# Attention products of each softmax in one run on TensorE: a transformer layer on one Trainium2 core

## The reference, cut to what matters

```
x = x + attn(layernorm(x))              # 16 heads of 32, rotary, causal softmax
x = x + cross(layernorm(x), ctx_2048)   # 16 heads of 32, int8-like rounding of the input and output projections
x = x + experts(layernorm(x))           # 64 experts, the best 8 for each token, 128 places in each
```

```
att = softmax(q @ k.T / sqrt(32));  y = att @ v      # for each of 32 sequences and 16 heads
```

## Time and profile before

| | us |
|---|---|
| median of 3 runs | 1783.19 |
| the three runs | 1784.44, 1783.19, 1775.75 |
| span of the profiled execution | 1569.0 |
| TensorE busy in it | 1406.8 |
| VectorE busy | 1168.0 |
| ScalarE busy | 971.5 |
| GpSimd busy | 673.1 |

### The profile page before, as it was taken

How to read it: one execution, slowest core, us unless ns; L and a number is a source line. 1 busy time by engine, 2 the same in 40 slices (tenths; PEclk the granted TensorE clock), 3 DMA queues, 4 the chain that set the end, 5 groups by cost and what they waited for, 6 DMA issues and landing times.

```text
span 1569.0 us, 35603 instructions
## 1 busy us (share of the span) xinstructions
PE 1406.8 (90%) x10963; PEld 1063.2 (68%) x10996; DVE 1168.0 (74%) x3111; ACT 971.5 (62%) x3345; POOL 673.1 (43%) x654
## 2 busy tenths in 40 slices
PE   3699999999999999999999999998619887888895
PEld 2467777777777777777777777776516565655573
DVE  5678889998999989999899999889524444444453
ACT  3357777777777777777777777777504333333342
POOL 0012444444444344453444534544343544555566
PEclk9799999999999999999999999999759999999997
DMA  9861332322111100111010111000597999999964
GB/s 283 347 237 35 131 125 101 105 98 107 66 46 45 34 27 27 34 34 40 27 27 27 34 43 30 27 21 21 191 331 214 292 249 287 281 276 281 261 99 51
DMA packets 159738, 195.81 MB, mean 125 GB/s; under 512 B 39541, under 2 KB 121845, under 8 KB 159680
## 3 DMA queue, kind: packets, MB, share of 16 engines
q1 hardware_dynamic: 120768, 157.27, 30.9%
q0 software_dynamic: 38912, 37.87, 11.8%
HBM read 127.60 MB, written 130.29 MB: 164 GB/s over the span
## 4 chain that ended last, share of the span: by engine, by line
PE 65%; DMA 23%; issue 5%; DVE 4%; ACT 1%; POOL 1%; SPq 1%; POOLq 0%; DVEq 0%
PE bank L502 33%; DMA out<-x,slots 20%; PE bank L527 7%; PE bank L484 7%; PE bank L520 5%; PE bank L534 4%; PE bank L508 3%; PE bank L540 2%; PE bank L515 2%; DMA x_in<-in_x 1%; PE bank L489 1%; DMA wide_b<-in_xkT_w 1%; POOL routed L1753 1%; DMA probsT<-in_oT_w 1%; ACT probs L966 1%
## 5 line engine op out<-in xcount | busy, mean ns | idle before, releaser
L966 ACT ACTIVATE probs<-bank,small 128x128 f32<-128x128 f32 x1024 | 362.1, 377 | 51.0 <-DVE small L1269 47.8
L1753 POOL DMA_INDIRECT routed<-row,slots x248 | 252.7, 1019 | 133.8 <-issue 74.0
L1822 POOL DMA_INDIRECT out<-x,slots x128 | 199.3, 1557 | 197.6 <-DMA out<-x,slots 137.4
L1718 POOL TENSOR_TENSOR small<-small,half 128x1 f32<-128x1 f32 x96 | 54.4, 567 | 523.3 <-DVE small L1241 523.3
L966 ACT ACTIVATION_READ_ACCUMULATOR probs<-bank,small 128x1 f32 x1024 | 220.7, 216 | 0.0
L960 ACT ACTIVATE probsT<-bank 128x512 f32<-128x512 f32 x256 | 144.1, 611 | 89.1 <-PE bank L527 89.1
L1269 DVE TENSOR_REDUCE small<-bank 128x4 f32<-128x512 f32 x256 | 166.7, 682 | 35.4 <-PE bank L520 35.4
L527 PE MATMUL bank<-idf,probs 128*128 128x128 f32 x1024 | 147.2, 277 | 2.4 <-ACT probs L966 2.4
L1673 DVE TENSOR_SCALAR slots<-pairs 128x1 uint32<-128x1 f32 x128 | 13.7, 149 | 174.7 <-DMA out<-x,slots 171.1
L527 PEld LDWEIGHTS bank<-idf,probs 128*128 128x128 f32 x1024 | 122.2, 144 | 26.8 <-DVE probs L1278 3.5
L1199 ACT ACTIVATE xn<-bank 128x192 f32<-128x192 f32 x64 | 21.3, 332 | 146.4 <-PE bank L906 146.4
(11 more groups left out here) (242 smaller groups left out, 3843.4 us busy)
## 6 DMA issues: line engine op xcount, KB each, us to landing
w_gate_up<-in_w_gate SPq DMA_DIRECT2D x128, 192.0 KB, 3.8
w_gate_up<-in_w_up SPq DMA_DIRECT2D x128, 192.0 KB, 4.0
w_down<-in_w_down SPq DMA_DIRECT2D x128, 192.0 KB, 4.4
routed<-empty_row SPq DMA_DIRECT2D x4, 5120.0 KB, 22.8
x_in<-in_x SPq DMA_DIRECT2D x32, 256.0 KB, 2.6
ctx_sb<-in_ctxT_in SPq DMA_DIRECT2D x32, 256.0 KB, 3.0
x_res<-in_x SPq DMA_DIRECT2D x32, 256.0 KB, 2.6
out<-x SPq DMA_DIRECT2D x32, 256.0 KB, 2.0
```

What stands on the lines that cost most here:

```text
L966: last = act.activation(probs[:, g, j * P:(j + 1) * P], bank[:, b, j * P:(j + 1) * P], ACT.Exp, bias=negated[:, h:h + 1], **({"accum_out": ...
L1753: pool.indirect_dma_start(routed, bass.IndirectOffsetOnAxis(ap=slots_of(m)[:, k:k + 1], axis=0), row_of(m)[:, :], None, bounds_check=SLOTS ...
L1822: pool.indirect_dma_start(out.rearrange("b p (h c) -> (b p h) c", h=2), bass.IndirectOffsetOnAxis(ap=place_of[k % 2][:, half_:half_ + 1], ...
```

## The change

Two calls in TensorE's list change their place. Every instruction, wait and buffer stays as it is.

```
                 if has(cur - 5):
                     positions(cur - 5)
-                if has(cur - 4):
-                    weigh_cross_1(cur - 4)
                 if has(cur - 2):
                     turn_queries(cur - 2)
                 if has(cur - 1):
                     turn_x(cur - 1)
+                if has(cur - 4):
+                    weigh_cross_1(cur - 4)
                 if has(cur - 4):
                     weigh_cross_3(cur - 4)
...
                 if has(cur - 2):
                     turn_probs_3(cur - 2)
-                if has(cur - 2):
-                    weigh_1(cur - 2)
                 if has(cur - 1):
                     keys_c(cur - 1)
+                if has(cur - 2):
+                    weigh_1(cur - 2)
                 if has(cur - 2):
                     weigh_3(cur - 2)
```

More of the change, by code:

```diff
@@ L811, in body @@
                     turn_probs_3(cur - 2)
+                if has(cur - 1):
+                    keys_c(cur - 1)
                 if has(cur - 2):
                     weigh_1(cur - 2)
-                if has(cur - 1):
-                    keys_c(cur - 1)
                 if has(cur - 2):
```

## The result

| | before | after |
|---|---|---|
| median, us | 1782.49 | 1689.35 |
| lowest to highest, us | 1775.75 to 1784.44 | 1683.13 to 1697.39 |
| ratio to before, 95% interval | | 0.9484 [0.9448, 0.9520] |
| span of the profiled execution, us | 1569.0 | 1695.5 |
| time of that execution, us | not given | 1697.39 |

Yet its profiled span is 126 us longer than that of before. The table holds the contradiction that the experiments have to resolve: here 1.9 us lie around the span, where the forecast had put 214.2.

What follows compares the result with a forecast made beforehand. TensorE, busy 90% of the span, was taken to bound the kernel. Cross-attention 30 x 0.21 = 6.3 us and self-attention 29 x 0.11 = 3.2 us gave 9.5 us less: 1773.7 us, range 1764 to 1783.

Steps and rivals of the forecast that it cites:

- so 214.2 us lie around it, which I leave as they are: Whole kernel: median 1783.19 us less profiled span 1569.0 us, taken as time around the span that the change leaves alone.
- The run of 32 products: Each softmax's products on TensorE: one run of 32 in place of 8 and 24, taking 1.02 us.
- Self-attention: TensorE's self-attention: transposes 0.41, `keys_c` 1.12, product run 1.02 us; 2.55 instead of 2.86, 0.31 us less a turn.
- The new wait behind the rotation: TensorE's bank 4 transposes wait 0.20 us for VectorE's rotation, leaving 0.11 us a turn of the self-attention's 0.31.
- Cross-attention: From second position product to `xk_sb` transposes: 2.09 instead of 2.30 us, 0.21 saved; step to first transpose 0.11, bounds 0.03 and 0.12.
- Order of waits: `turn_queries` and `weigh_3` now wait for fourth copies; cover of 0.55 and 0.46 us, so no cost.
- The period: One turn of the attention loop: 32.93 us less 0.32, so 32.61 us.
- The first rival: No new wait for VectorE's rotation, so both savings stay whole: 15.6 us less, 1767.6 us; chance 0.17.
- the rival in which the cross part brings nothing: Cross-attention saves nothing, only the rotation's slack counts: 3.2 us less, 1780.0 us, or 0 by the overlap rule; chance 0.19.
- the rule on weight loads: On TensorE, a weight load overlaps running matmuls only when the row group differs; by it the change saves 0.
- the third rival: Where the prediction said the weight-load rule keeps a chance; third in its list is the slower case, chance 0.06.
- the slower one: ScalarE's fourth copy comes late and TensorE stands at `turn_queries`: 5.4 us more, 1788.6 us; chance 0.06.

Runs made afterwards that it cites:

- the kernel before again: The kernel before, unaltered, run again to profile a usual execution: 1781.97 us, ratio 1.0012, span 1779.5 us.
- self half: The kernel before with only `weigh_1` moved behind `keys_c`, the cross-attention's order as before: 1780.40 us, ratio 1.0002.
- cross half: The kernel before with only `weigh_cross_1` moved behind `turn_queries` and `turn_x`, the self-attention's order as before: 1705.36 us, ratio 0.9600.
- later scatters: The kernel before with eight tiny memsets on GpSimd ahead of each turn's scatters: 1770.84 us, ratio 0.9950, where signals were late.

## Why the prediction was wrong

**The step that failed** is the one in the sum that reads "so 214.2 us lie around it, which I leave as they are". They don't lie around the span: what lies around it is 1.9 us in the changed kernel's profiled run, and 1.8 us in that of the kernel before again (1781.32 - 1779.5). The profile of before was of an execution without late signals (span 1569.0, as in the sessions at 1569 to 1572), while the runs of before, 1783, had them. Nearly all of the 214.2 us was thus time lost inside the loop over the tiles: a turn of 40.84 us where the profile had 32.93. I named the difference and then treated it as a constant, though nothing showed what it held. All that follows from the profile is true of 1569.0 us; on it I built a difference for a kernel whose turn takes about 40.4 us on average. That what is worth something is "the spacing of TensorE's instructions, until another engine's result comes too late" is right as a sentence, but its condition was not met in the runs: another engine's result did come too late, in nearly every turn. None of the rivals had late signals in it either.

**The terms of the sum** can be judged where signals are on time. The changed kernel, by time, cross part, self part and bank 4:

```profile
803.35 0.19 PE L546 MATMUL bank<-chosen_before,ones_b 128*128 128x64 bf16 x1
803.38 0.63 PE L484 MATMUL bank<-idf,roped 128*128 128x128 f32 x4
...
804.38 1.08 PE L534 MATMUL bank<-probsT,xv_sb 128*32 128x128 f32 x32
805.39 0.66 PE L484 MATMUL bank<-idf,xk_sb 128*128 128x128 f32 x4
...
821.18 0.66 PE L527 MATMUL bank<-idf,probs 128*128 128x128 f32 x4
821.59 1.16 PE L502 MATMUL bank<-w_k_hi,xT_lo 128*128 128x512 f32 x4
822.69 1.08 PE L534 MATMUL bank<-probsT,v_sb 128*32 128x128 f32 x32
823.70 0.50 PE L502 MATMUL bank<-w_v_hi,xT_hi 128*128 128x512 f32 x1
...
829.95 1.23 DVE L1307 TENSOR_TENSOR roped<-roped,wide_a 128x1024 f32<-128x1024 f32 x1
...
830.26 1.00 PE L540 MATMUL bank<-router_w,x3T 128*128 128x64 f32 x8
...
831.23 0.42 PEld L527 LDWEIGHTS bank<-idf,probs 128*128 128x128 f32 x4
...
831.23 0.66 PE L527 MATMUL bank<-idf,probs 128*128 128x128 f32 x4
```

Of before, the two groups around bank 4 that were not shown:

```profile
839.76 1.00 PE L540 MATMUL bank<-router_w,x3T 128*128 128x64 f32 x8
...
840.60 0.61 PE L527 MATMUL bank<-idf,probs 128*128 128x128 f32 x4
```

- *The run of 32 products:* forecast 1.02 us, measured 805.39 - 804.38 = 1.01 and 823.70 - 822.69 = 1.01. Right.
- *Self-attention:* transposes 0.41 (forecast 0.41), `keys_c` 1.10 (1.12), in all 2.52 us against 2.86, 0.34 saved; forecast 0.31.
- *The new wait behind the rotation:* the load stands 831.23 - 829.95 = 1.28 us behind the start of the rotation's last operation, exactly as in the earlier trace rows. The step from the router's products to the transposes grew from 0.84 to 0.97 us, so the wait is 0.13 us; forecast 0.20. The self half keeps 0.21 us a turn, not 0.11.
- *Cross-attention:* the step from position product to transpose is 803.38 - 803.35 = 0.03 us, the lower of my two bounds; I had taken 0.11. In all 2.04 us against 2.30, 0.26 saved; forecast 0.21.
- *Order of waits:* TensorE shows no idle time at `turn_queries` or `weigh_3`. Right.
- *The period:* 32.50 us (`xk_sb` transposes at 675.39 and 707.89 in the same profile), forecast 32.61; so 0.43 us saved in a turn and not 0.32. The parts above add up to 0.47, and 0.04 us of that is not accounted for.

Together 30 x 0.26 + 29 x 0.21 = 13.9 us; the medians of that session give 13.4, those without scatters 14.3, and the forecast was 9.5. So the mechanism was right where signals are on time, and the size was too small, mostly by the step behind the position products. The first rival's condition (no new wait) did not hold, though its 15.6 us is near; the rival in which the cross part brings nothing fell (the prediction files the rule on weight loads under "the third rival", but it is worked out under this one, the second); the slower one never came.

**The other 80 us** come from less lateness. In the wait rows, the maxima's "remote" idle went from 113.7 to 82.4 us (the windows hold fewer turns of the slower kernel, so per operation still more) and the copy's from 70.3 to 59.2; with it went stalls of TensorE and stretches at the lower clock (turns such as that of 35.70 us with clock 1.00 are seen in the changed kernel and its cross half, not in the kernel before).

The length of a turn follows the copy of the turned input, and not the maxima. In the kernel before it starts 6.8 to 7.4 us behind its transposes in 22 of 24 turns, 2.2 to 2.3 us behind the start of the last scatter, and turns take 39 to 41.6 us. In the self half and with later scatters the maxima are earlier (median 3.3 and 3.4 us instead of 3.9), the copy is not (mostly 7.3 to 7.4), and nothing or 0.5% is gained. In the changed kernel the copy's signal gets out before the last scatter in many turns: 4.7 to 4.8 us in 11 of 26, and these take 35.7 to 37.0 us; in the four with 7.6 us a turn takes 39.7 to 40.6 us.

Shown is that the scatters cause the lateness, that the cross half alone carries the gain, and that the changed kernel with gaps in the burst is free of most of the rest (1604.78 where 1689 was measured without them, in another session). Not shown is how the cross half does it. That it starts the scatters later against TensorE's signals fits all starts seen (0.05, 0.22 and 0.25 us: 40.4 to 40.7 us a turn; 0.31 and 0.48: 37.5 to 37.8), but the kernel meant to separate this from the order of the products reached only 0.25. The start alone can't be all: in the changed kernel it is 0.47 to 0.50 us behind the transposes in nearly every turn, while the copy is late by 4.7 us in one and 7.6 in another. Open too is what a session has that holds signals back, and whether the issuing or the transfers of the scatters do it.

## What to carry to other kernels

Before a profile's rows are priced, its span must agree with the time of usual runs to a few microseconds; where it doesn't, the profile may be of another regime, and a difference worked out in it holds for that regime alone. An engine with idle time is not harmless for that: a burst of indirect transfers from GpSimd, entirely off the critical path, cost 227 us through the signals of TensorE where a session held them back, and about 7 us where not. Look for readers that wait for "remote" or "an unknown queue" in a kernel of one core, and try gaps in the burst before moving it as a block, for a block takes its lateness along.

## What the runs showed of the hardware

- TensorE's completion signals can come 2 to 7 us late while GpSimd's indirect scatters, issued 1.28 us apart, are under way: VectorE's maxima started 3.93 us behind the scores' end and ScalarE's copy 7.1 us behind its transposes. Without scatters the maxima started 0.06 us behind. The scatters cost about 7 us in one kind of session (1569.23 us with, 1562.62 without, from two sessions) and 227 us in the other.
- The kind did not change within any of the seven sessions (9 to 20 executions of the kernel before in each), and it is not bound to a chip: the same chip gave 1569, 1572 and 1779 us for the same kernel.
- Some 0.4 us of tiny memsets between scatters, which spread their starts from 1.28 to 1.5 us, lowered the time by 9.7% against the kernel before, where the change alone had lowered it by 5.2% in another session.
- After stalls of several microseconds TensorE's granted clock averaged 0.91 to 0.92 over a turn. In the turn of the kernel before shown above its busy time was 36.24 us, against about 32.9 us in a turn with signals on time: some 3.3 of the 7.9 us by which that turn is longer.
- Bf16 position products (64 columns) and float32 transposes stand only 0.03 us apart, while the edge of a run of 32-column products costs 0.14 us and more.
